# A three-attention kernel: the context products of a slot issued in pairs, at fewer places

## The reference, cut to what matters

```python
# layer 0 (causal, with a relative bias); layer 3 the same without bias and mask
att = jnp.einsum('bhtd,bhsd->bhts', q, k) / np.sqrt(D)
att = att + bias[None]
att = jnp.where(causal[None, None], -jnp.inf, att)
att = jax.nn.softmax(att, axis=-1)
out = jnp.einsum('bhts,bhsd->bhtd', att, v)
# layer 1: the scores are a product of two
logits = jnp.einsum('bnhr,bmhr->bhnm', q1, k1) * jnp.einsum('bnhr,bmhr->bhnm', q2, k2) * SCALE
```

## Time and profile before

| what | value |
|---|---|
| median of 3 runs | 1598.15 us |
| lowest and highest | 1591.09 and 1600.19 us |
| span of the profiled execution | 1592.6 us |
| TensorE busy | 1295.5 us, 81% of the span |
| VectorE, ScalarE, GpSimd busy | 864.5, 634.7 and 486.5 us |
| mean granted TensorE clock | 0.89 of full speed |

### The profile page before, as it was taken

How to read it: one execution, slowest core, us unless ns; L and a number is a source line. 1 busy time by engine, 2 the same in 40 slices (tenths; PEclk the granted TensorE clock), 3 DMA queues, 4 the chain that set the end, 5 groups by cost and what they waited for, 6 DMA issues and landing times. The chain is left out here.

```text
span 1592.6 us, 26296 instructions
## 1 busy us (share of the span) xinstructions
PE 1295.5 (81%) x9753; PEld 756.8 (48%) x9761; DVE 864.5 (54%) x2261; ACT 634.7 (40%) x1318; POOL 486.5 (31%) x550
## 2 busy tenths in 40 slices
PE   3996899886978858999996976683896899999498
PEld 2563555553555435555553552442574233333277
DVE  4046556552035557667643548684137888783305
ACT  1321444442323224665553214241234477676043
POOL 5553012112230066665400001125472121212443
PEclk9996999997997978999997988685897599998699
DMA  6842422101640016655524500001434211200334
GB/s 129 183 99 80 105 71 67 33 19 49 178 123 10 1 58 200 181 170 158 158 61 53 81 7 1 0 9 53 113 108 114 65 62 41 77 28 15 83 109 124
DMA packets 152201, 130.46 MB, mean 82 GB/s; under 512 B 19197, under 2 KB 137865, under 8 KB 152080
## 3 DMA queue, kind: packets, MB, share of 16 engines
q1 hardware_dynamic: 143136, 116.15, 27.5%
q0 software_dynamic: 6304, 11.37, 2.2%
q10 hardware_dynamic: 2640, 1.36, 0.6%
HBM read 81.86 MB, written 47.69 MB: 81 GB/s over the span
## 5 line engine op out<-in xcount | busy, mean ns | idle before, releaser
L2462 DVE TENSOR_REDUCE att_maxima<-psum 128x2 f32<-128x1024 f32 (+3 forms) x384 | 355.5, 951 | 178.5 <-PE psum L2101 76.7
L2343 ACT ACTIVATE att_probs<-psum 128x512 f32<-128x512 f32 (+1 forms) x640 | 320.7, 554 | 275.3 <-PE psum L2141 108.2
L108 POOL TENSOR_TENSOR rstd<-var_eps,neg_half 128x4 f32<-128x4 f32 x44 | 45.1, 1025 | 556.9 <-DVE var_eps L99 556.6
L2121 PE MATMUL psum<-att_queries,att_keys 50*128 50x512 bf16 (+3 forms) x512 | 128.4, 362 | 30.2 <-ACT att_probs L2343 22.4
L1044 POOL DMA_INDIRECT returned<-moe_out,moe_slot_tokens x101 | 101.6, 1005 | 129.0 <-DVE moe_out L972 103.6
L838 ACT ACTIVATE moe_hidden<-psum,moe_b 128x320 f32<-128x320 f32 (+1 forms) x128 | 77.8, 608 | 129.1 <-PE psum L751 127.1
L172 PE MATMUL psum<-ident,normalised_rows 128*128 128x128 f32 x192 | 42.9, 365 | 96.3 <-DVE normalised_rows L117 73.9
L758 PE MATMUL psum<-moe_w,moe_hidden 128*128 128x128 f32 (+1 forms) x784 | 109.5, 286 | 0.0
L2081 PE MATMUL psum<-att_keys,att_queries 48*128 48x512 bf16 (+3 forms) x512 | 95.3, 382 | 14.5 <-DVE att_maxima L2462 14.2
L751 PE MATMUL psum<-moe_slot_columns,moe_w 128*128 128x320 f32 (+1 forms) x256 | 99.9, 534 | 2.9 <-ACT moe_slot_columns L833 2.9
L758 PEld LDWEIGHTS psum<-moe_w,moe_hidden 128*128 128x128 f32 (+1 forms) x784 | 91.0, 183 | 14.9 <-issue 7.2
(11 more groups left out here) (296 smaller groups left out, 2321.1 us busy)
## 6 DMA issues: line engine op xcount, KB each, us to landing
score_terms<-att_parts SPq DMA_DIRECT2D x44, 384.0 KB, 3.2
moe_w<-l_w SPq DMA_DIRECT2D x64, 256.0 KB
moe_back<-returned SPq DMA_DIRECT2D x24, 256.0 KB, 4.2
att_queries<-score_terms SPq DMA_DIRECT2D x64, 96.0 KB
att_keys<-score_terms SPq DMA_DIRECT2D x64, 96.0 KB
att_queries<-score_terms SPq DMA_DIRECT2D x16, 384.0 KB, 4.3
att_keys<-score_terms SPq DMA_DIRECT2D x16, 384.0 KB, 5.4
dispatched<-untaken SPq DMA_DIRECT2D x2, 2064.0 KB, 24.5
```

The costliest lines, as they stand in the source:

```text
L2121: mm = nc.tensor.matmul(dst, k_op[half, i, p, key], q_op[half, i, p, query], start=c0 == 0, stop=kind == 3, skip_group_check=True)
L2343: nc.scalar.activation(probs[:, G % 2, 2 * p + r, unit_at[u]:unit_at[u] + w], g.psum[:, cols_bank + r, 0:w], ACT.Exp).then_inc(probs_ready, 1)
L2462: ins = nc.vector.tensor_reduce(maxima[:, G % 2, t, 2 * p:2 * p + 2], g.psum[:, rows_bank(k):rows_bank(k) + 2, c0:c0 + w], axis=AX, op=ALU ...
```

## The change

`context_at`, which gave one step for a position, now gives a tuple of steps, and the loop issues them one behind the other.

```diff
-    context_at = {1: 0, 2: 1, 4: 2, 5: 3} if causal else {x: x for x in range(X)}
+    context_at = {1: (0,), 2: (1,), 5: (2, 3)} if causal else {x: (x - 1, x) for x in range(1, X, 2)}
...
-                    if x in context_at and 0 <= n - 1 < NG:
-                        if n == 1 and x == 1 and not split:
+                    for step in context_at.get(x, ()) if 0 <= n - 1 < NG else ():
+                        if n == 1 and step == 0 and not split:
                             bank_free(other_last, o_copied, 1)
-                        (context_step if causal else context_half)(n - 1, context_at[x])
+                        (context_step if causal else context_half)(n - 1, step)
```

## The result

The changed kernel takes 1612.52 us in the median of 4 runs (1605.38 to 1619.97), the kernel before 1595.98 (1591.09 to 1600.19): a ratio of 1.0106, 95% interval 1.0064 to 1.0149, or +17 us. In the experiments the same kernel ran twice more, beside the kernel before on the same chip each time: 1.0087 (1.0061 to 1.0113) and 1.0073 (1.0035 to 1.0110), that is +14 and +12 us. So it is slower by 0.7 to 1.1%. The profiled execution has a span of 1603.6 us against 1592.6; its own time was 1605.38.

The account below looks back on a forecast made before the run. The prediction took a loop between TensorE and ScalarE to bound the kernel. Layers 0, 1 and 3 gave 2.9 + 3.1 + 2.6 = +8.6 us, a median of 1606.5 us, range 1594 to 1622.

Parts of the forecast that it names:

- forecast case: Whole kernel: the costed layers sum to +8.6 us, median 1606.5 us, own range 1600 to 1612; chance 0.60.
- rival 3: Slots 14 and 15 of layer 3: the clock falls earlier, 1615 us, up to +20 more if ahead; chance 0.17.
- the wait of L2121: Sign in layer 3: the columns' wait on ScalarE's `att_probs` grows from 22.4 us by 20 or more.
- the granted clock of layer 3: Sign in layer 3: a granted clock below 0.92 shows that the clock falls.
- What bounds the kernel: Attention: a loop between TensorE and ScalarE; columns r = 1 start 1.55 us behind the previous position's columns.
- A visit: Context shape: each visit less saves TensorE 0.22 us; 90 visits in layers 0, 1 and 3, 19.8 us.
- rival 1: Whole kernel: TensorE is the bound, so saved visits are a gain, about 1578 to 1588 us; chance 0.09.
- Layer 0: Moved steps: -0.7 with projections, +1.0 with `turn_rows`, +2.6 with no turn at x = 4; sum +2.9 us.
- I take 0.12 off: Layer 0, six slots with a projection at x = 4: 0.57 goes, 0.43 comes back; 0.12 less each, -0.7 us.
- Layer 1: Moved step: +0.09 in slots 1 to 10, 0.43 lost in slots 11 to 15; sum +3.1 us.
- Layer 3: Turnless pair 3.10 us against 2.67, slot 12.54; -1 where x = 4 is filled, +3.6 elsewhere; sum +2.6 us.
- Rival 2: Layer 3: regular turns hide at even positions, 0.6 us from each of ten slots; 1595 to 1600 us; chance 0.14.

Follow-up runs that it names:

- e2: Pairs of context steps in layer 3 only, layers 0 and 1 as in the kernel before: 1.0041 against the kernel before, +6.5 us.
- e1_again: The changed kernel run once more, unaltered, for a second profile, against the kernel before on the same chip: 1.0087, +14 us.
- e8: The changed kernel run a third time, unaltered, against the kernel before on the same chip: 1.0073, +12 us.
- e6: Layer 3 with pairs at odd positions plus each even step also issued at its even position, 64 steps more: 1.0093 against the kernel before, +14.5 us.
- e5: Layer 3 in pairs at even positions, on the side of the turns, layers 0 and 1 as before: 1.0137 against the kernel before, +21 us.
- e3: Pairs in layers 0 and 1 only, layer 3 as in the kernel before: 1.0017 against the kernel before, +2.7 us.
- e9_spread2: Kernel before with the four steps of layers 0 and 1 at x = 0, 1, 3, 4, layer 3 unchanged: 0.9948 against the kernel before.
- e7: Layers 0 and 1 stepping at x = 0, 1, 3, 4; pairs only where long turns fill emptied places in layers 0 and 3: 0.9948 against kernel before.
- e10: Second run of: steps at x = 0, 1, 3, 4 in layers 0 and 1, pairs only at turn-filled places; 0.9909 against kernel before, -14.5 us.

## Why the prediction was right

The direction, the mechanism and most lengths were as written; the size was not: +8.6 us forecast, +12 to +17 measured. The first median, 1612.52, lies inside the range of 1594 to 1622 but just above the forecast case's own 1600 to 1612, next to the 1615 of rival 3 (the clock). Two of the signs named in advance spoke against the plain forecast case: the wait of L2121 grew by 15.4 us, not by 20 or more, and the granted clock of layer 3 was 0.91, below the 0.92 that was to show rival 3. (Over slots 2 to 17 it is 0.91 there and in e2, 0.94 in e1_again and e8, and 0.94 to 0.96 with single steps.)

- **What bounds the kernel.** Right. The loop of columns, exponentials and columns takes 1.55 us whatever TensorE does, shown by e6, where a whole step added in the gap leaves the pair at 3.10.
- **A visit.** 0.22 us was right in size: two steps take 1.00 us and one 0.57. That all of it is paid by the path (rival 1, and the rule on the drain alone) is refuted by e2 and e5: equal numbers of visits, +6.5 and +21 us. By the Trainium skill ("TensorEngine Tiling (Array Packing)", section "Tiling Modes") changing the mode drains the engine, and the trace agrees that a visit has a price, 0.14 us beside its streaming. The visit that was saved in layer 3 had stood where TensorE waited anyway.
- **Layer 0.** The term "I take 0.12 off" was too small. Slots with a projection gained 0.3 (13.31 against 13.59 to 13.63), since the longer visit at x = 5 also covers the exponentials before the next x = 0. Slots without a turn lost 0.3 instead of 0.43 (13.32 against 12.98 to 13.06) and slots 5 and 9 with `turn_rows` 0.12 instead of 0.32, for the same reason. Forecast +2.9, profiled +0.7 between slots 2 and 17. This total is the lowest of four: in e1_again, e3 and e8 the same placement takes 196.7 to 197.7 us, over 3 us of it in slots 15 and 16 (11.1 to 11.3 and 3.6 to 3.8 us at clocks of 0.76 to 0.80, where the first profile has 8.8 and 3.0 at 1.00; e2, with the old placement, has 8.4 and 3.0 at 1.00, and 196.2 in all).
- **Layer 1.** Right: +0.12 in slots 2 to 4 against +0.09 forecast, +0.43 in slots 12 and 13 as forecast, +2.4 in all against 3.1. The total holds some luck: slot 6 alone went from 17.31 us (clock 0.90) to 15.58 (1.00), and is back at 17.20 in e8, while slots 15 and 16 lost 1.7 at a lower clock.
- **Layer 3.** The pair (3.10) and the slot (12.44 against 12.54 forecast) were right, and the loss of slots 10, 12 and 14, without a projection, (+0.3 to +0.9) within the bounds. The sum failed: +2.6 was taken, 5.7 is the mean over four profiles each, 7.2 the first profile. By slots (slot 1, with +0.6 in the sum, lies outside this stretch):

  | slots of layer 3 | taken, us | mean of four against four, us |
  |---|---|---|
  | 2 to 12 | +1.0 | -1.0 |
  | 13 | -0.1 | +1.4 |
  | 14 | +0.6 | +0.9 |
  | 15 | +0.6 | +3.8 |
  | 16 | 0 | +0.6 |

  The term that was mis-sized is that of slot 15. It takes 14.6 to 15.9 us at a granted clock of 0.62 to 0.64 in all four profiles with pairs; with single steps it takes 13.3 at 0.67 in two and 10.0 to 10.2 at 1.00 in two. That is rival 3 at the place where it was put, one of the last two slots with scores. The late start of ScalarE in slot 11, which made 2.5 us of the first profile's 7.2, adds nothing on the mean (15.7 us against 16.0). Where ScalarE starts late, the old order had a context step to issue and the new one has none: the columns wait 2.50 us in slot 11 and 2.28 in slot 13 of the first profile, against 1.08 at most in those of the kernel before.
- **Rival 2** (turns win) was partly true: slots 2 to 9 together are 2 us shorter. It is outweighed by slots 10 to 16, 9.1 us longer in the first profile: they have fewer turns, and 11, 13 and 15 are at a low clock.

The clock of the changed kernel late in layer 3, against the earlier trace rows:

```profile
1426.00:1446.00 20.00, 17.42 (x166) 6.74 (x166) 15.98 (x26) 14.02 (x26) 3.89 (x4) 0.98 0.04 13
1446.00:1455.00 9.00, 7.92 (x50) 3.62 (x51) 5.91 (x21) 5.31 (x11) 0.08 (x1) 0.62 0.02 5
1455.00:1471.00 16.00, 12.29 (x128) 4.99 (x127) 3.12 (x14) 11.90 (x22) 6.20 (x6) 1.00 0.06 19
1471.00:1485.00 14.00, 12.63 (x84) 5.37 (x84) 1.40 (x7) 5.63 (x11) 0.00 (x0) 0.51 0.00 0
```

There is a fall at 1446, behind a wait of 2.28 us on ScalarE, that the first profile of the kernel before does not have (e3, with single steps in layer 3, has one in that slot: 15.34 us at 0.89). Pairs alone do not bring the clock down at once: from 1455 to 1471 TensorE is busy in 12.3 of 16 us and the clock stays at 1.00. The fall at the end, in slot 15, comes behind a wait of 1.00 us. Slot 15 in the kernel before, in e9_spread2 (single steps in layer 3, too) and in the changed kernel:

```profile
1456.58:1469.93 13.35, 12.21 (x89) 4.83 (x87) 1.12 (x5) 7.79 (x15) 2.65 (x3) 0.67 0.04 11
1447.18:1457.22 10.04, 8.95 (x89) 3.74 (x87) 1.12 (x5) 7.68 (x15) 2.65 (x3) 1.00 0.05 15
1467.14:1482.94 15.80, 12.96 (x89) 5.18 (x87) 1.12 (x5) 7.90 (x15) 2.27 (x2) 0.62 0.03 9
```

How far each fall adds to the time, and whether the pairs bring it on in slot 15, was not tried by itself; it rests on four profiles against four. In slot 11 the price, 18.45 against 12.99 and 12.93 us, holds the length of the late start too.

## What to carry to other kernels

When two engines alternate over single buffers, small independent work belongs into the latency of the loop: one piece behind each hand-over that is waited for, and none where a turn already stands. Batching such pieces to save a mode switch saves a fixed 0.2 us and can expose up to twice that; batch only where something else of at least the same length fills the place that is emptied. Before batching, look in the timeline at the places that already have nothing in them: if the next instruction waits there today, it will wait at the new empty places too. And count a loss slot by slot over several profiles of each kernel: in one profile, a single late start can look like the cause of what another slot loses every time.

## What the runs showed of the hardware

- ScalarE and VectorE, together or one of them, sometimes start late on work that TensorE has done ("remote" in the waits, 1.0 to 3.1 us). In layer 3 these late starts stand in slots 9, 11 and 13, about 7 to 9 us behind the turn at x = 2, with single steps and with pairs alike; the profiles of e5, e6 and e7, all on one chip, have none there. No row shows the cause.
- Behind a wait of 2.50 us TensorE's granted clock was at its lower level (1.2 GHz), and a pair of context steps took 1.87 us instead of 1.00. The length of one wait does not decide it: in slot 15 of layer 3 the clock fell behind a wait of 1.04 us in the kernel before, and stayed at 1.00 behind one of 1.03 in e3.
- On the chip of e5 to e7 the kernel before took 1563.93 us, on the others 1592 to 1596, while undisturbed slots have the same length to 0.01 us (12.90 in layer 1 on both). One placement took 179.31 us for layer 3 there (e7, the clock at 1.00 in all slots but two) and 190.66 on another chip (e10, below 1.00 in seven): the profiles differ in late starts and falls of the clock, not in undisturbed slots.
